# Edge stage of a graph attention kernel: GpSimd only gathers, VectorE weighs four heads of every pair

## What is computed

```python
Q, K, V = (x @ Wq), (x @ Wk), (x @ Wv)          # (N, H, d), H = 8, d = 64
score = exp(clip(einsum('ehd,ehd->eh', K[src], Q[dst]) / 8, -5, 5))[..., None]
wV = segment_sum(V[src] * score, dst, N)
Z  = segment_sum(score, dst, N)
h = x + wV / (Z + 1e-6)
out = layernorm(x + (h - mean(h, 0)) * rsqrt(var(h, 0) + 1e-5) * gamma + beta)
```

## Time and profile before

| | |
|---|---|
| median of 3 runs | 1907.17 us (1906.17 to 1910.18) |
| the profiled execution | 1908.01 us, of which the span of its instructions is 1906.1 us |
| first and last multiplication of the edge stage (L795, 440 of them) | 463.3 and 1752.3 us |
| TensorE's granted clock over the span | 0.994 |

### The profile page before, as it was taken

One profiled execution on the slowest core, in us unless ns is written; L12 is line 12 of the kernel. 1 busy time (PEld: TensorE's weight loads), 2 busy tenths in 40 slices (PEclk: granted clock), 3 DMA queues, 4 the chain that ended last, 5 costly groups with the idle time before them and its releaser, 6 DMA issues.

```text
span 1906.1 us, 41424 instructions
## 1 busy us (share of the span) xinstructions
PE 1861.6 (98%) x7904; PEld 1362.2 (71%) x8014; DVE 1697.0 (89%) x2454; ACT 1367.5 (72%) x4602; POOL 1291.3 (68%) x1473
## 2 busy tenths in 40 slices
PE   7999999998999999999999999999999999999897
PEld 4555555554888888878888888888888888887333
DVE  6677755644999999999999999999999999999888
ACT  0002000002999999999999999999999999998857
POOL 0205666103777888788888888888888888885677
PEclk9999999999999999999999999999999999999999
DMA  5547788546999999999999999999999999999307
GB/s 183 162 151 250 288 319 274 186 161 231 357 358 356 362 367 358 346 351 368 368 356 353 352 366 369 354 355 355 366 361 358 360 355 365 370 358 370 122 33 287
DMA packets 184521, 589.09 MB, mean 309 GB/s; under 512 B 28480, under 2 KB 30240, under 8 KB 184480
## 3 DMA queue, kind: packets, MB, share of 16 engines
q0 software_dynamic: 135904, 465.14, 65.8%
q1 hardware_dynamic: 45120, 121.69, 17.8%
q10 hardware_dynamic: 3456, 1.78, 0.3%
HBM read 535.27 MB, written 78.91 MB: 322 GB/s over the span
## 4 chain that ended last, share of the span: by engine, by line
PE 74%; DVE 16%; issue 4%; DMA 4%; ACT 1%; POOL 1%; SPq 0%; DVEq 0%; ACTq 0%; POOLq 0%
PE acc L939 29%; PE places L342 22%; PE q_ps L923 17%; DVE kv L795 6%; DVE raw L806 5%; DMA kv<-kv_d,idx 2%; PE mm_ps L949 2%; PE banks L1151 1%; DVE stats L1288 1%; DVE agg L1281 1%; PE mm_ps L951 1%; PE places L402 1%; DMA q_tile<-xb_d 1%; POOL kv L751 1%; PE banks L1142 1%
## 5 line engine op out<-in xcount | busy, mean ns | idle before, releaser
L751 POOL DMA_INDIRECT kv<-kv_d,idx x880 | 887.0, 1008 | 339.2 <-issue 204.8
L846 ACT ACTIVATE kv<-kv 128x64 f32<-128x64 f32 x3520 | 889.0, 335 | 14.3
L939 PE MATMUL acc<-kv,mm_sb 128*128 128x260 f32 x3520 | 845.6, 383 | 4.1 <-POOL kv L714 2.2
L939 PEld LDWEIGHTS acc<-kv,mm_sb 128*128 128x128 f32 x3520 | 654.3, 190 | 137.9 <-issue 32.8
L923 PE MATMUL q_ps<-q_tile,mm_sb 128*128 x1760 | 559.2, 439 | 5.6 <-DVE kv L795 4.9
L795 DVE TENSOR_TENSOR kv<-q_ps,kv 128x1024 f32<-128x1024 f32 x440 | 536.1, 1218 | 14.0 <-PE q_ps L923 7.0
L806 DVE TENSOR_REDUCE raw<-kv 128x16 f32<-128x1024 f32 x440 | 532.2, 1210 | 0.0
L923 PEld LDWEIGHTS q_ps<-q_tile,mm_sb 128*128 128x128 f32 x1760 | 328.6, 189 | 74.4 <-DVE kv L795 20.8
L714 DVE TENSOR_TENSOR kv<-kv 128x384 f32<-128x384 f32 (+1 forms) x440 | 271.6, 617 | 0.1
L857 ACT ACTIVATE mm_sb<-mm_ps,less 128x1024 fp32r<-128x1024 f32 x220 | 241.2, 1096 | 13.1 <-remote 10.1
L435 ACT COPY p<-places 128x768 f32<-128x768 f32 x23 | 18.4, 798 | 243.5 <-PE places L342 243.5
(11 more groups left out here) (171 smaller groups left out, 1358.6 us busy)
## 6 DMA issues: line engine op xcount, KB each, us to landing
q_tile<-q_d SPq DMA_DIRECT2D x49, 512.0 KB, 7.2
kv<-kv_d,idx POOLq DMA_INDIRECT x880, 6.2
kv_d<-kv_a SPq DMA_DIRECT2D x25, 512.0 KB, 5.5
xb<-in_x POOLq DMA_DIRECT2D x49, 256.0 KB, 4.3
xb_d<-xb POOLq DMA_DIRECT2D x49, 256.0 KB, 3.7
out_rows<-agg SPq DMA_DIRECT2D x49, 256.0 KB, 2.1
x_sb<-in_xT SPq DMA_DIRECT2D x24, 512.0 KB, 7.9
q_d<-q_a SPq DMA_DIRECT2D x24, 512.0 KB, 4.1
```

The costliest lines, as they stand in the source:

```text
L751: pool.indirect_dma_start(kv[:, s, u, 0:2 * DIM], None, kv_d, bass.IndirectOffsetOnAxis(idx[:, s, u:u + 1], 0), bounds_check=N_NODES - 1, ...
L846: return act.activation(v, v, ACT.Copy, scale=kv[:, s, u, 2 * DIM + h:2 * DIM + h + 1])
L939: last = pe.matmul(acc[:, bass.ds(par, 1), DIM - (1 - n) * HALF:DIM + n * HALF], m, kv[:, sc, u, DIM + n * HALF:DIM + (n + 1) * HALF], sta ...
```

## The change

GpSimd weighs no head any more; VectorE weighs heads 4 to 7 of every pair and counts that in one new semaphore, `s_w`. On it GpSimd's gather of pair q waits for the weighing of pair q-6, in place of the wait on `s_qx`, and TensorE's sums wait for it besides `s_v`, which ScalarE alone counts now. Indices are copied for two pairs at a time, in every even step. GpSimd's loop has one round less and its unrolled end one more.

```diff
-IDX_PAIRS = 4
+IDX_PAIRS = 2
...
-        POOL_LAG = 5
+        GATHER_LAG = 6
...
                 if u == 0:
                     if s % IDX_PAIRS == 0:
                         wait_apart(pool, s_idx[s // IDX_PAIRS], fills)
-                    wait_apart(pool, s_qx, q + 5 - RING)
...
             def step(q, s, fills):
-                p = q - POOL_LAG
-                sp, fp = at(s, fills, -POOL_LAG)
+                if there(q):
+                    wait_apart(pool, s_w, q + 1 - GATHER_LAG)
                 if there(q):
                     gather(q, s, fills, 0)
                 if there(q + 2) and s % IDX_PAIRS == IDX_PAIRS - 2:
                     index(q + 2, *at(s, fills, 2))
                 if there(q):
                     gather(q, s, fills, 1)
-                if s % 2 and there(p):
-                    wait_apart(pool, s_exp[sp], fp)
-                    weigh(pool, sp, HEADS - POOL_HEADS, POOL_HEADS).then_inc(s_v[sp], 1)
...
-                    weigh(dve, s2, ACT_HEADS, HEADS - ACT_HEADS - (POOL_HEADS if s % 2 == 0 else 0)).then_inc(s_v[s2], 1)
+                    weigh(dve, s2, ACT_HEADS, HEADS - ACT_HEADS).then_inc(s_w, 1)
...
-                    pe.wait_ge(s_v[sc], (2 if sc % 2 else 3) * fc)
+                    pe.wait_ge(s_v[sc], fc)
+                    pe.wait_ge(s_w, c + 1)
```

More of the change, by code:

```diff
@@ L655, in attend @@
         s_mm = [sem(f"s_mm{n}") for n in range(RING // 2)]
-        s_t_first = sem("s_t_first")
+        s_t_first, s_w = sem("s_t_first"), sem("s_w")
         s_lb = [soft[f"s_lb{g}"] for g in range(RING // LB_PAIRS)]
@@ L774, in _ @@
                 step(s, s, 1)
-            with nc.Fori(1, ROUNDS, engines=[pool.engine], head_slot={pool.engine: POOL_HEAD}) as i:
+            with nc.Fori(1, ROUNDS - 1, engines=[pool.engine], head_slot={pool.engine: POOL_HEAD}) as i:
                 for s in range(RING):
                     step(i * RING + s, s, i + 1)
-            for q in range(ROUNDS * RING, PAIRS + POOL_LAG):
+            for q in range((ROUNDS - 1) * RING, PAIRS):
                 step(q, q % RING, q // RING + 1)
```

## The result

The change makes the kernel slower: 1952.72 us (median of 4 runs, 1948.81 to 1954.95) against 1907.41 us (4 runs, 1906.17 to 1910.18) on the same chip, a ratio of 1.0233 with a 95% interval of 1.0213 to 1.0254. The profiled execution took 1948.81 us, its span is 1947.0: 40.9 more than before. Slower was right. The 1920.5 us, and the range up to 1935, were not.

What follows compares the result with a forecast made beforehand. TensorE was taken to set the edge stage's pace by a hair over VectorE. Terms 13.2 - 3.1 - 1.5 + 5 = 13.6 us on 1908.0 gave 1921.6; adjusted to the median, 1920.5 us, range 1910 to 1935.

Steps and rivals of the forecast that it cites:

- VectorE's extra head: Edge stage: VectorE weighs four heads in every step, all steps become 2.935 us and VectorE passes TensorE; +13.2 us.
- GpSimd's weighing goes: Edge stage: TensorE's waits for GpSimd's weighing, and VectorE's `q_ps` waits taken as following from them, vanish; -3.1 us.
- Small delays: Edge stage: TensorE's small delays, up to 0.06 us in two steps, no longer reach VectorE; -1.5 us.
- The copies of indices: GpSimd in the edge stage: 110 more copies stay hidden, 5.3 us against VectorE's 5.87 for two steps; 0 us.
- The gathers' new wait: GpSimd's gathers: lead shrinks by 0.6 us, so a few rows land late; +5 us, bounds 0 and 20.
- a rule for the weighing that goes: VectorE's two-input and GpSimd's SBUF instructions exclude each other; removing GpSimd's weighing could give back up to 90 us; not summed.
- rival 1: Edge stage: gathers land late and VectorE waits for them, 20 us in place of 5; about 1936 us, chance 0.15.
- Rivals 2 and 3: No change that can be told, about 1910 us, chance 0.10; faster by VectorE's port, 1903 to 1908 us, chance 0.05.
- The sign: Whole kernel: slower than before by more than 3.8 us, chance 0.85, with VectorE becoming the bound.

Runs made afterwards that it cites:

- i_idx2: The kernel before with index copies of two pairs instead of four; 1.0014 of the kernel before, on a slower chip.
- m_order: The change with GpSimd waiting for indices before the weighing and copying indices after the pair's second gather; 1.0519 of the kernel before, on a slower chip.
- m_order4: `m_order` with index copies of four pairs instead of two; 1.0671 of the kernel before, on a slower chip.
- b_wait: The kernel before with only the gathers' new wait on `s_w`; GpSimd still weighs, indices four pairs at a time; 0.9991 of the kernel before, slower chip.
- c_qx: The change in full, except that gathers wait on `s_qx` as before; 0.9985 of the kernel before, on a slower chip.
- d_reduce: The change with VectorE's weighing of heads 4 to 7 replaced by a one-input reduction of the same values; 1.0553 of the kernel before, slower chip.
- p_both: The change with a second wait ahead of each pair's gathers, on `s_qx` for pair q-3; 1.0013 of the kernel before, slower chip.
- e_change: The change itself, unaltered, run again on a slower chip; 1.0549 of the kernel before there.

## Why the prediction was wrong, point by point

The terms, against the first chip's traces:

- **VectorE's extra head, +13.2.** Right in mechanism and nearly in size. The steps are 2.93 to 2.94 us in the median, and 439 x 2.935 is 1288.5 as forecast. Without the waits, the stage after is 1328.8 - 31.3 - 2.5 = 1295.0, which is 6.5 over that.
- **GpSimd's weighing goes, -3.1.** VectorE's waits for `q_ps` fell from 7.0 to 2.5 us: -4.5. TensorE never waits for GpSimd now.
- **Small delays, -1.5.** Wrong in sign: 2.4 us before, 6.5 after, so +4.1. This is the remainder of the stage once the other terms are named, so the sum below closes by construction.
- **The copies of indices, 0.** By themselves nearly so: `i_idx2` has 1.0014. But they are held too, and then push the gathers, and that belongs to the next term. On chip 14 two copies for one made 1.0549 of 1.0386, on chip 3, with GpSimd's order altered, they did not (`m_order`, `m_order4`).
- **The gathers' new wait, +5. This step failed**: 31.3 - 4.3 = +27.0. Together 13.2 - 4.5 + 4.1 + 27.0 = 39.8.

Two things are in those 27. The first is that I kept 1.0 us for a gather and 0.20 for a copy, with a message-to-gather time of 0.83, and put nothing for their being held. The rows had a sign of it: the longest gather in the earlier trace rows took 1498 ns, in a kernel whose second gathers seldom started early in a weighing (3 of 410 held). The trace of after has 1.17 us from the weighing's end to the first gather in even slots and 1.51 in odd ones (medians), and the second gather ends 0.7 us later than that schedule in the median of all pairs, because of held copies and gathers. The lead of the second gather is 7.40 us in the median, not 7.5 to 7.7, against 8.26 before. That includes VectorE's own waits, which lengthen it; over stretches of six steps without a wait it is 6.8 us in even slots and 7.2 in odd ones; at pair 63 above it is 7.1 (644.70 to 651.82, when the multiplication was due). `b_wait`, `c_qx` and `d_reduce` show that the wait and the two-input weighing make the holding and that without it the schedule is the forecast one, and `m_order` that GpSimd's own order can undo it.

The Trainium skill, page "SBUF — State Buffer", section "Who interferes with whom", was already in the prediction as a rule for the weighing that goes. It speaks against the change as well: a GpSimd instruction that reads SBUF waits for the whole of a VectorE instruction with two inputs there, and the copies and gathers read indices there. The trace agrees (0.64 to 0.82 us for a copy of 0.20). That section of the Trainium skill also tells of a probe in which such a VectorE instruction did not stall a DMA, and infers that generating the descriptors needs the other side of the shared port. For indirect gathers the measurement here decides otherwise, with up to 1.54 us in place of 0.99.

The second is that I priced late rows from the spread of landings over all pairs: one pair in seven late by 0.3 us as the upper bound. Landings are not spread by chance. Where the 512 KB load is issued within 2 us of a pair's second gather, its rows take 7.3 to 7.9 us in the median, in after as before (there 7.7 to 8.0 for 39 of 44). Before, the lead of 8.1 to 8.3 covered that: 3 of 44 such pairs were late, 1.0 us. After, 30 of 69 are, 26.6 us (600 to 1720 us). So the loss comes at three loads in four (41 in that stretch), by 0.9 us each: fewer pairs than in my bound, and each three times as late. That is rival 1 by mechanism, with 27 us where it had 20; it had a chance of 0.15.

How much of it is holding? If from each late pair's wait its own second gather's delay against the unheld schedule is taken off, 5 to 6 us of some 30 remain (38 pairs; those over 0.1 us late). By this reckoning the shorter lead alone would have been near my +5, and holding is the rest. It is a reckoning on the trace, and it takes for granted that rows land earlier by as much as they are asked for earlier. `m_order` would have tested it, but never ran on a chip like the first, and on the others the late messages outweigh it. So it is shown that holding costs the second gather 0.7 to 0.8 us of lead, and that late rows cost the 27 us; how much of the 27 the holding makes stays argued.

**Rivals 2 and 3** fell: neither did the lead hold, nor did VectorE's instructions get shorter worth speaking of (multiplication 1217 against 1223 ns, the four-head weighing 686 against 682). **The sign** was right for the reason given, but only a third of the loss has that reason.

## What to carry to other kernels

A wait does more than delay: it ties one engine's phase to another's. Work out where in the other engine's step each instruction behind the wait will start, and what it shares there; that the wait is satisfied with time to spare says nothing on it. Price late transfers at the moments when another transfer is issued beside them, not from the distribution over all of them. And a wait that looks redundant can still set the time: with `s_qx` awaited again, `p_both` came back from 1.055 to 1.001 on the slower chips. Last, an experiment settles a share of the loss only on a chip that loses time in the same way.

## What the runs showed of the hardware that I had not expected

- GpSimd's indirect gather (0.99 us) that starts inside a VectorE multiplication of two SBUF operands (0.69 us) ends 0.87 us behind that one's end, up to 1.54 us in all; one that started ahead of it takes 0.99 to 1.02. A copy of indices (0.20 us) that meets it ends 0.04 behind it. With a reduction in its place (one input, 0.68 us) the longest gather between 600 and 1700 us is 1.03 and the longest copy 0.21 us.
- The same kernel takes 1907 us on one chip and 2086 to 2109 on three others, at a granted clock of 0.99 on both. On those, TensorE's message behind a group of matmuls comes 1 us late in the typical late case of the kernel before, and up to 5.0 in the variants; on the first, never over 0.02. One wait of GpSimd more or less was worth 5% there.
- Behind the long waits TensorE's clock falls: `e_change` has 191 us of its edge stage at 1.2 GHz, the kernel before 10 on the same chip number.
